# Turning the gated product on VectorE in 32 x 32 blocks instead of by fp32 transposes on TensorE, and projecting it with matmuls of 32 rows by 32 columns

## The chip, the cores and the metric

One core of one Trainium2 chip runs the whole kernel. The metric is the device time in microseconds from the first to the last instruction of that core with what lies around them. The median of three runs before the change is 772.9 us (772.75 to 773.51).

## The reference

Two layers of the same form run one after the other over x of shape (4, 32, 128, 128), with weights of their own:

```
def layer(x, W_in, W_dw, fft_weight, W_out):      # x is the group-normed input, one group per channel
    xm = einsum('bchw,oc->bohw', x, W_in)           # 32 -> 3 * 85 channels
    x_spatial, x_freq, x_gate = split(xm, 3, axis=1)
    out_spatial = depthwise_conv3x3(x_spatial, W_dw)
    out_freq = irfft2(rfft2(8x8 patches of x_freq) * fft_weight)
    x_fused = gelu(x_gate) * (out_spatial + out_freq)
    return einsum('bchw,oc->bohw', x_fused, W_out)  # 85 -> 32 channels
x = x + layer(gn(x), ...)    # layer 0
x = x + layer(gn(x), ...)    # layer 1
```

The change touches only the last lines of a layer: the product `x_fused`, which lies with pixels on the partitions, has to be turned so that its 85 channels lie there, and is then contracted with `W_out`, whose result is added to x.

## The kernel before

The image is cut in four bands of 32 columns (Q = 4), which lie with their 32 channels on the 128 partitions: partition 32 q + c is channel c of band q. A strip is 8 columns wide and 128 rows high; layer, batch and strip give 32 strips. A tile is 16 x 8 = 128 pixels of each band, 8 tiles to a strip, 256 in all. The engines walk through the same `steps()`, one tile to a step, with a prologue and a drain, and each engine has its order written out by hand in its own block; semaphores named `s_...` join them. Nothing plans the order at run time.

In step i TensorE does, in this order (L584 to L656): `conv(i, 0)` (seven matmuls that project and convolve band 0 of tile i, into one of two banks `ps_s`), the four fp32 transposes of tile i-2 into bank `ps_ft` (L594), every fourth step the output projection of four tiles (L616), the gate matmuls (L549) mixed with the other three bands' convolutions (L543), `turn` and `transform` of a later pair of tiles for the spectrum (L511, L523, L524), the projection of the spectrum of tile i+2 (`ps_z`, L639), and at the end two inverse-transform matmuls that complete the sum of tile i (L654, L656).

VectorE in step i: the product of the gate `g` and the sum in `ps_s` for tile i-1 (L1097, it signals `s_f`), in every fourth step the low part of a group's spectrum (L1045), in steps of certain numbers a normalization (L1005) or the low half of a strip's operands (`lo_part`, L1029, which waits for ScalarE's high half, L707), the weighting of the spectrum of tile i+2 (`y32`, L1120, needs `s_z`), and in every fourth step the residual sum out of `ps_o` (L1133), in layer 0 with statistics behind it (L967). ScalarE copies `ps_ft` to SBUF (L765, into one of 8 slots of `turned_results`), does the gelu (L770), moves the turned pixels (L727), makes the high half of `y32` (L777) and the high halves of the operands (L707). GpSimd makes the low half of `y32` (L844) and issues the DMAs that bring the spectrum into its stacked layout (`load_spectrum`, three DMAs for each of four bands q per group of four tiles, L425). SyncE issues the loads of the stacked operands.

TensorE waits for `s_f` of tile i-2 before `conv(i, 0)` since `ps_s` has two banks, for `s_y` of tile i+1 before `ps_z` is written, and for `s_gelu` of tile i-1 before the gate. The projection takes `wo` (85 x 32, fp32) as the stationary operand and four tiles of 128 pixels (512 columns) as the moving one, once per band, with band q's result in partitions 32 q to 32 q + 31 of `ps_o`. The factor `osc` that undoes the scaling of the weights is applied in the residual sum.

Of the kernel before, what the change touches and what calls it, by code (L numbers as in the profile page):

```python
# [47 lines left out]
PAIR, GROUP = 2, 4  # L48

# [49 lines left out]
def build(nc, x_in, edges_in, w_raw, w_fft, w_out, waves, squares, fold, sums, y_out):  # L99
    ctx = ExitStack()  # L100
    with ctx:
# [27 lines left out]
        turned_results = sb("turned_results", [128, 2 * OUT * Q * 128])  # L129
        raw = [turned_results[:, 0:12 * HID], yo[1][:, 0:12 * HID]]  # L130

        last = turned_results[0:KH, (2 * OUT - 1) * Q * 128:]
        fold_sb, fft = last[:, 0:128], [last[:, 128 + HID * i:128 + HID * (i + 1)] for i in range(LAYERS)]
        ones = turned_results[0:3, (2 * OUT - 1) * Q * 128 + 384:2 * OUT * Q * 128]
# [16 lines left out]
        wo = [sb(f"wo{i}", [HID, C]) for i in range(LAYERS)]  # L151
# [26 lines left out]
        ft = turned_results[0:HID, :].rearrange("p (t q n) -> p t q n", q=Q, n=128)  # L178
# [4 lines left out]
        ps_xt, ps_x, ps_g, ps_z, ps_ft, ps_o = (bank(n) for n in ("ps_xt", "ps_x", "ps_g", "ps_z", "ps_ft", "ps_o"))  # L183
# [10 lines left out]
        s_wo = sem("s_wo")  # L194
        s_x0 = [sem(f"s_x0_{i}") for i in range(STRIPS)]
# [51 lines left out]
        s_xs = [sem(f"s_xs{i}") for i in range(HELD)]  # L247
        s_z = sem("s_z")
# [7 lines left out]
        s_ftp = sem("s_ftp")  # L256
        s_ft = sem("s_ft")
        s_o = sem("s_o")
        s_res = sem("s_res")
# [179 lines left out]
        def _(sp):  # L439
# [7 lines left out]
            for l in range(LAYERS):  # L447
                sp.dma_start(wo[l][:, :], w_out[l]).then_inc(s_wo, 16)
# [19 lines left out]
        def _(pe):  # L468
# [24 lines left out]
            pe.wait_ge(s_wo, 16 * LAYERS)  # L493
            pe.wait_ge(s_id16, 1)

            def warm(n):

                for _ in range(n):
                    mm(ps_ft[:, 0:256], bas, waves_sb[:, :, :].rearrange("p a n -> p (a n)"), start=True, stop=True)
# [53 lines left out]
            def spectra_loaded(h):  # L553
# [3 lines left out]
                elif h == 1:  # L557
                    for by in range(2):
                        pe.wait_ge(s_xs_first[1][by], 16 * 2 * 3)
                else:  # L560
                    pe.wait_ge(s_xs[h % HELD], 16 * 3 * Q * ((h - 2) // HELD + 1))
# [22 lines left out]
            for i in steps():  # L584
# [21 lines left out]
                if live(i, -6) and i % OUT == 2:  # L606
# [52 lines left out]
        def _(act):  # L659
# [70 lines left out]
            def hi_of_spectrum(h):  # L730
# [5 lines left out]
                elif h > 3:  # L736
                    act.wait_ge(s_xs[(h - 2) % HELD], 16 * 3 * Q * ((h - 4) // HELD + 1))
# [65 lines left out]
        def _(pool):  # L803
# [28 lines left out]
            for i in steps():  # L832
# [3 lines left out]
                for h in range((i + 4) // GROUP, (i + 7) // GROUP + 1):  # L836
                    for q in range(Q):
# [19 lines left out]
        def _(dve):  # L857
# [24 lines left out]
            def scales(l):  # L882
# [10 lines left out]
                v.tensor_scalar(osc[l][:, :], p2[:, l, 0:1], p2[:, l, 1:2], 1.0 / SS, ALU.mult, ALU.mult)  # L893
# [155 lines left out]
            v.memset(ones[:, :], 1.0)  # L1049
            link(v.memset(amax[:, :, :], 0.0))  # L1050
# [197 lines left out]
```

## Time and profile before

| | |
|---|---|
| median of three runs | 772.9 us (772.75 to 773.51) |
| profiled execution, its own time | 775.2 us |
| its span, first to last instruction | 773.4 us |
| mean granted TensorE clock | 0.985 |
| TensorE matmuls busy | 723.6 us, 94% |
| VectorE busy | 545.1 us, 70% |
| ScalarE busy | 572.5 us, 74% |
| GpSimd busy | 624.1 us, 81% |

Busy time is the union of the engine's instructions. Neighbouring instructions of one engine overlap by some tens of ns in the records, because the next one starts while the one before still drains; so the distance between two starts says what an instruction costs in a row of others, and its duration what it costs to one that waits for its result.

### The profile page before, as it was taken

To read this page: it belongs to the slowest core of one execution; us is meant where nothing else is said; L and a number is where in the kernel's file an instruction comes from. 1 tells how busy PE (TensorE), PEld (TensorE's weight loads), DVE (VectorE), ACT (ScalarE), POOL (GpSimd) and SP (SyncE) were. 2 spreads that over 40 slices of the span, in tenths; PEclk is the share of its full clock that TensorE was granted. 3 is DMA by queue.
4 is the path that set the end of the run, shared out by engine and by line. 5 is a ranking of instruction groups with operands and counts; after the bars stand their busy time and mean duration, and the time that the engine had idled before them with its cause. 6 is when DMAs were issued, how large, how long until landed. Compare 5 with 4: busy or idle time off the path is not lost.

```text
span 773.4 us, 32267 instructions
## 1 busy us (share of the span) xinstructions
PE 723.6 (94%) x12324; PEld 620.0 (80%) x12324; DVE 545.1 (70%) x957; ACT 572.5 (74%) x1087; POOL 624.1 (81%) x1071
## 2 busy tenths in 40 slices
PE   2589989999999999999999999999999999999997
PEld 1477778877888878888788888889888988898875
DVE  7578867878877876777777687666666676667543
ACT  1676667777787778878887778787778777877754
POOL 1977777888888898888888987988788888988871
PEclk9689999999999999999999999999999999999999
DMA  8676888787767765677766766877767777787741
GB/s 299 162 182 174 195 181 211 170 190 174 180 177 191 182 160 152 163 167 182 189 171 165 166 183 176 216 190 199 190 176 192 194 199 204 194 209 191 191 129 56
DMA packets 96259, 140.61 MB, mean 182 GB/s; under 512 B 32498, under 2 KB 34746, under 8 KB 95978
## 3 DMA queue, kind: packets, MB, share of 16 engines
q1 hardware_dynamic: 64390, 103.30, 51.6%
q0 software_dynamic: 25376, 26.75, 14.1%
q10 hardware_dynamic: 6340, 8.49, 4.3%
q8 instruction: 99, 1.62, 1.0%
q14 instruction: 54, 0.44, 0.2%
HBM read 10.81 MB, written 8.54 MB: 25 GB/s over the span
## 4 chain that ended last, share of the span: by engine, by line
PE 72%; DVE 7%; issue 6%; POOL 6%; DMA 5%; ACT 2%; SPq 1%; ACTq 0%; POOLq 0%; DVEq 0%
PE ps_s L543 29%; PE ps_ft L594 12%; PE ps_o L616 7%; PE ps_g L549 5%; DMA xs<-xf 4%; PE ps_z L639 4%; PE ps_s L656 4%; PE ps_s L654 4%; PE ps_xt L511 3%; POOL xs L425 2%; PE ps_x L523 2%; PE ps_x L524 2%; POOL yl L844 1%; DVE y L1120 1%; POOL stack L305 1%
## 5 line engine op out<-in xcount | busy, mean ns | idle before, releaser
L543 PE MATMUL ps_s<-cw,stack 128*128 128x85 f16 (+1 forms) x7168 | 407.3, 203 | 1.8 <-DMA stack<-parts 1.6
L425 POOL DMA_DIRECT2D xs<-xf x757 | 385.2, 513 | 15.7 <-PE ps_z L639 12.5
L543 PEld LDWEIGHTS ps_s<-cw,stack 128*128 128x128 f16 (+1 forms) x7168 | 352.8, 99 | 27.4 <-issue 1.9
L844 POOL TENSOR_TENSOR yl<-y,yh 128x340 f16<-128x340 f32 x256 | 219.0, 856 | 105.2 <-ACT yh L777 103.1
L1120 DVE TENSOR_TENSOR y<-ps_z,weff 128x340 f32<-128x340 f32 x256 | 129.6, 506 | 136.8 <-PE ps_z L639 129.9
L777 ACT ACTIVATE yh<-y 128x340 f16<-128x340 f32 x256 | 124.6, 487 | 135.2 <-DVE y L1120 118.1
L1029 DVE TENSOR_TENSOR parts<-xn,parts 128x1024 f16<-128x1024 f32 (+2 forms) x99 | 126.9, 1284 | 63.8 <-ACT parts L707 63.5
L594 PE MATMUL ps_ft<-squares_sb,g 128*85 128x128 f32 x1024 | 163.4, 282 | 0.8 <-ACT turned_results L765 0.8
L765 ACT ACTIVATE turned_results<-ps_ft 85x512 f32<-85x512 f32 x256 | 149.3, 583 | 16.7 <-issue 10.0
L770 ACT ACTIVATE g<-ps_g,gsc 128x340 f32<-128x340 f32 x256 | 137.2, 536 | 18.7 <-PE ps_g L549 18.2
L1097 DVE TENSOR_TENSOR g<-ps_s,g 128x340 f32<-128x340 f32 x256 | 128.2, 501 | 11.0 <-PE ps_s L656 8.1
L549 PEld LDWEIGHTS ps_g<-pw,stack 128*128 128x128 f16 x1024 | 82.6, 98 | 55.2 <-issue 52.8
L549 PE MATMUL ps_g<-pw,stack 128*128 128x85 f16 x1024 | 125.0, 205 | 0.0
L594 PEld LDWEIGHTS ps_ft<-squares_sb,g 128*85 128x85 f32 x1024 | 115.3, 155 | 2.1 <-DVE g L1097 1.0
L707 ACT ACTIVATE parts<-xn 128x1024 f16<-128x1024 f32 (+2 forms) x99 | 100.3, 1017 | 14.4 <-DVE xn L1013 12.4
L639 PE MATMUL ps_z<-pw,xs 96*128 96x85 f16 x1024 | 81.5, 203 | 12.4 <-DMA xs<-xf 12.0
L654 PE MATMUL ps_s<-yh,waves 128*128 128x340 f16 x256 | 79.7, 311 | 0.0
L727 ACT ACTIVATE xt<-ps_xt 128x512 f16<-128x512 f32 x127 | 74.7, 588 | 6.7 <-PE ps_xt L511 4.2
L656 PE MATMUL ps_s<-yl,waves 128*128 128x340 f16 x256 | 79.0, 309 | 0.6 <-POOL yl L844 0.6
L616 PE MATMUL ps_o<-turned_results,wo 85*32 85x512 f32 x512 | 68.2, 605 | 1.3 <-ACT turned_results L765 0.7
L639 PEld LDWEIGHTS ps_z<-pw,xs 96*128 96x128 f16 x1024 | 54.9, 98 | 14.2 <-DMA xs<-xf 7.1
L523 PE MATMUL ps_x<-waves,xt 128*128 128x128 f16 x254 | 42.9, 222 | 13.7 <-DVE xf L1045 10.4
(108 smaller groups left out, 548.0 us busy)
## 6 DMA issues: line engine op xcount, KB each, us to landing
stack<-parts SPq DMA_DIRECT2D x496, 130.0 KB, 3.6
xs<-xf POOLq DMA_DIRECT2D x757, 32.0 KB, 2.8
out_y<-yo SPq DMA_DIRECT2D x16, 512.0 KB, 3.1
stack<-parts SPq DMA_DIRECT2D x93, 64.5 KB, 2.9
stack<-parts SPq DMA_DIRECT2D x93, 64.0 KB, 2.8
x<-in_x SPq DMA_DIRECT2D x16, 256.0 KB, 6.0
stack<-parts ACTq DMA_DIRECT2D x62, 65.0 KB, 3.8
stack<-parts SPq DMA_DIRECT2D x62, 65.0 KB, 2.8
```

The source lines that it names most:

```text
L425: eng.dma_start(xs[C * k:C * k + C, h % HELD, q, :], xf[C * q:C * q + C, h % 2, SPECTRA[k], :]).then_inc(loaded, 16)
L543: mm(ps_s[i % 2][:, HID * q:HID * (q + 1)], pixels(kind, i, q, dy, rows), w[0:rows, m, :], start=(q == 0 and m == 0), stop=False)
L549: t = mm(ps_g[:, HID * q:HID * (q + 1)], pixels(A, i, q, 0), pw[layer(i)][:, 1, :], start=(q == 0), stop=(q == Q - 1))
L594: t = nc.tensor.transpose(ps_ft[0:HID, q * 128:(q + 1) * 128], g[:, k, HID * q:HID * (q + 1)], id32)
L639: z = mm(ps_z[:, HID * q:HID * (q + 1)], xs[:, (i + 2) // GROUP % HELD, q, col:col + 128], pw[layer(i + 2)][0:3 * C, 0, :], start=(q == 0) ...
L765: nc.scalar.activation(ft[:, (i - 2) % (2 * OUT), :, :].rearrange("p q n -> p (q n)"), ps_ft[0:HID, 0:Q * 128], ACT.Copy).then_inc(s_ft, 1)
L770: nc.scalar.activation(g[:, i % 2, :], ps_g[:, 0:GC], ACT.Gelu, scale=gsc[layer(i)][:, 0:1]).then_inc(s_gelu, 1)
L777: nc.scalar.activation(yh[:, i % 2, :], y32[:, i % 2, :], ACT.Copy).then_inc(s_yh, 1)
L844: nc.gpsimd.tensor_tensor(yl[:, k, :], y32[:, k, :], yh[:, k, :], ALU.subtract).then_inc(s_yl, 1)
L1029: v.tensor_tensor(part[:, LO, rows], xn[:, rows, 1 + dx:1 + dx + TW], part[:, HI, rows], ALU.subtract).then_inc(s_xl, 1)
L1097: v.tensor_tensor(g[:, k, :], ps_s[k][:, 0:GC], g[:, k, :], ALU.mult).then_inc(s_f, 1)
L1120: v.tensor_tensor(y32[:, k, :].rearrange("p (q o) -> p q o", q=Q), ps_z[:, 0:GC].rearrange("p (q o) -> p q o", q=Q), weff[layer(i + 2)][:, ...
```

## The change

The product goes to a buffer `f` of its own, whose rows are padded from 85 to 96 = 3 x 32 channels. VectorE turns it there in square blocks of 32 x 32 into `ft` and signals `s_ft`; the four fp32 transposes, bank `ps_ft` and ScalarE's copy are gone. Each 32-row group of `ft` then holds 32 channels of one block for 32 pixels, so the output is projected by matmuls of 32 rows and 32 columns: two bank halves, three blocks that are summed, four bands, and two rounds n between which TensorE waits for its own first round (`s_o_half`). `W_out` is laid out anew on the host in blocks and repeated four times, the factor `osc` goes into it once (`s_wo_scaled`), the residual sum becomes two plain additions, one per bank. The fourth of the four band loads of the spectrum is issued by ScalarE instead of GpSimd.

```diff
@@ TensorE
-                if live(i, -2):
-                    k = i % 2
-                    need(pe, s_f, i - 1)
-                    need(pe, s_ft, i - 2)
-                    for q in range(Q):
-                        t = nc.tensor.transpose(ps_ft[0:HID, q * 128:(q + 1) * 128],
-                                                g[:, k, HID * q:HID * (q + 1)], id32)
-                    t.then_inc(s_ftp, 1)
...
-                    for q in range(Q):
-                        o = mm(ps_o[C * q:C * q + C, :], wo[layer(tile)][:, :], ft[:, k:k + OUT, q, :],
-                               start=True, stop=True)
-                    o.then_inc(s_o, 1)
+                    if tile % LT == 0:
+                        pe.wait_ge(s_wo_scaled, layer(tile) + 1)
+                    for n in range(2):
+                        if n == 1:
+                            pe.wait_ge(s_o_half, tile // OUT + 1)
+                        for block in range(BLOCKS):
+                            for half in range(2):
+                                rows = slice(BLOCK * (2 * half + n), BLOCK * (2 * half + n + 1))
+                                out = ps_os[half][:, 0:OUT * 2 * BLOCK].rearrange("p (t n x) -> p t n x", n=2, x=BLOCK)
+                                for q in range(Q):
+                                    o = mm(out[C * q:C * q + C, :, n, :], wo[layer(tile)][rows, block, :],
+                                           ft[rows, k:k + OUT, q, block, :],
+                                           start=(block == 0), stop=(block == BLOCKS - 1))
+                        o.then_inc((s_o_half, s_o)[n], 1)
@@ ScalarE
-                if live(i, -2):
-                    need(act, s_ftp, i - 1)
-                    need(act, s_o, (i - 2 - 2 * OUT) // OUT + 1)
-                    nc.scalar.activation(ft[:, (i - 2) % (2 * OUT), :, :].rearrange("p q n -> p (q n)"), ps_ft[0:HID, 0:Q * 128],
-                                         ACT.Copy).then_inc(s_ft, 1)
                 if live(i, 0):
                     need(act, s_gate, i + 1)
-                    need(act, s_ftp, i - 1)
+                    need(act, s_f, i - 1)
...
+                for h in range(2, GROUPS_OF_TILES):
+                    if loads_at(h, Q - 1) == i:
+                        load_spectrum(act, h, Q - 1, s_xs_act[h % HELD])
@@ GpSimd
-                    for q in range(Q):
+                    for q in range(Q - 1):
@@ VectorE
+                dve.wait_ge(s_wo, 16 * LAYERS)
+                v.tensor_scalar(wo[l], wo[l], osc[l][:, 0:1], None, ALU.mult).then_inc(s_wo_scaled, 1)
...
-                    v.tensor_tensor(g[:, k, :], ps_s[k][:, 0:GC], g[:, k, :], ALU.mult).then_inc(s_f, 1)
+                    v.tensor_tensor(f[:, k, :, 0:HID], ps_s[k][:, 0:GC].rearrange("p (q o) -> p q o", q=Q),
+                                    g[:, k, :].rearrange("p (q o) -> p q o", q=Q), ALU.mult).then_inc(s_f, 1)
                 if i in leaving:
                     lo_of_spectrum(leaving[i])
+                if live(i, -1):
+                    dve.wait_ge(s_f, i)
+                    need(dve, s_o, (i - 1 - 2 * OUT) // OUT + 1)
+                    v.transpose(ft[:, (i - 1) % (2 * OUT), :, :, :].rearrange("p q b n -> p (q b n)"),
+                                f[:, (i - 1) % 2, :, :].rearrange("p q h -> p (q h)")).then_inc(s_ft, 1)
...
-                    v.scalar_tensor_tensor(xv if l + 1 < LAYERS else staging,
-                                           ps_o[:, :].rearrange("p (r w) -> p r w", w=TW),
-                                           osc[l][:, 0:1], xv, ALU.mult, ALU.add).then_inc(s_res, 1)
+                    for half in range(2):
+                        ...
+                        o = v.tensor_tensor(new, ps_os[half][...], old, ALU.add)
+                    o.then_inc(s_res, 1)
```

## Rows read from the trace of the kernel before

**Rows 1.** Page, part 1: busy us (share of the span) xinstructions of each engine.
```profile
PE 723.6 (94%) x12324; PEld 620.0 (80%) x12324; DVE 545.1 (70%) x957; ACT 572.5 (74%) x1087; POOL 624.1 (81%) x1071
```
**Rows 2.** Page, part 4: the chain of waits, share of the span by engine.
```profile
PE 72%; DVE 7%; issue 6%; POOL 6%; DMA 5%; ACT 2%; SPq 1%; ACTq 0%; POOLq 0%; DVEq 0%
```
**Rows 3.** Busy time by stretch: length, PE, PEld, DVE, ACT, POOL, PE clock, DMA.
```profile
58.30:227.80 169.50, 158.77 (x2700) 135.35 (x2696) 134.66 (x241) 123.90 (x235) 136.22 (x236) 0.99 0.79 187
227.80:409.30 181.50, 177.24 (x3077) 152.30 (x3074) 134.94 (x230) 145.59 (x279) 157.26 (x268) 1.00 0.69 169
409.30:584.90 175.60, 173.27 (x3027) 149.87 (x3024) 121.97 (x201) 136.08 (x260) 149.12 (x255) 1.00 0.72 187
584.90:760.00 175.10, 173.94 (x3056) 150.33 (x3054) 110.15 (x186) 132.63 (x254) 143.73 (x246) 1.00 0.69 185
```
**Rows 4.** Timeline of PE, 404.99 to 409.37: start, us, group.
```profile
404.99 0.45 PE L543 MATMUL ps_s<-cw,stack 128*128 128x85 f16 x7
405.27 0.64 PE L594 MATMUL ps_ft<-squares_sb,g 128*85 128x128 f32 x4
405.75 0.24 PE L549 MATMUL ps_g<-pw,stack 128*128 128x85 f16 x2
...
407.71 0.64 PE L594 MATMUL ps_ft<-squares_sb,g 128*85 128x128 f32 x4
408.28 1.07 PE L616 MATMUL ps_o<-turned_results,wo 85*32 85x512 f32 x8
409.28 0.25 PE L549 MATMUL ps_g<-pw,stack 128*128 128x85 f16 x2
```
**Rows 5.** Timeline of PE again, cut off at 408.31 us.
```profile
408.28 0.64 PE L616 MATMUL ps_o<-turned_results,wo 85*32 85x512 f32 x4
```
**Rows 6.** Timeline of DVE, 399.88 to 402.81 us.
```profile
399.88 0.74 DVE L1133 SCALAR_TENSOR_TENSOR x<-ps_o,osc,x 128x512 f32<-128x512 f32 x1
400.66 0.69 DVE L967 BATCH_NORM_STATS2 st<-x 128x6 f32<-128x512 f32 x1
401.27 0.49 DVE L1097 TENSOR_TENSOR g<-ps_s,g 128x340 f32<-128x340 f32 x1
401.68 1.22 DVE L1029 TENSOR_TENSOR parts<-xn,parts 128x1024 f16<-128x1024 f32 x1
402.81 0.50 DVE L1120 TENSOR_TENSOR y<-ps_z,weff 128x340 f32<-128x340 f32 x1
```
**Rows 7.** One DVE line: ns min/median/max of each form.
```profile
L925 DVE COPY cw<-vh x1: 294/294/294, 24.2 to 24.2; 96x510 f16<-96x510 f16 x1
```
**Rows 8.** Waits, 58.3 to 227.8: engine line, releaser: us, times, longest.
```profile
DVE y L1120 <- PE ps_z L639: 21.3, 18, 3.3
DVE parts L1029 <- ACT parts L707: 10.4, 13, 1.2
```
**Rows 9.** Waits, 227.8 to 409.3 us.
```profile
DVE parts L1029 <- ACT parts L707: 13.9, 16, 1.1
```
**Rows 10.** Waits, 409.3 to 584.9 us.
```profile
DVE parts L1029 <- ACT parts L707: 19.0, 22, 1.1
```
**Rows 11.** Waits, 584.9 to 760 us.
```profile
DVE y L1120 <- PE ps_z L639: 44.4, 37, 3.4
DVE parts L1029 <- ACT parts L707: 17.2, 19, 1.1
```
**Rows 12.** Lines of ACT and POOL: xcount, busy us, mean ns, idle before.
```profile
L765 ACT ACTIVATE turned_results<-ps_ft 85x512 f32<-85x512 f32 x256 | 149.3, 583 | 16.7 <-issue 10.0 <-PE ps_ft L594 4.6 <-PE ps_o L616 1.7
L425 POOL DMA_DIRECT2D xs<-xf x757 | 385.2, 513 | 15.7 <-PE ps_z L639 12.5 <-issue 2.3 <-ACT xf L738 0.7
```
**Rows 13.** DMA issues, 130 to 730 us: KB each, median us to landing.
```profile
xs<-xf POOLq DMA_DIRECT2D x642, 32.0 KB, 2.8
stack<-parts ACTq DMA_DIRECT2D x54, 65.0 KB, 3.7
```
**Rows 14.** Timeline of ACT and its queue at 403.4 us.
```profile
403.35 0.49 ACT L777 ACTIVATE yh<-y 128x340 f16<-128x340 f32 x1
403.41 0.51 ACTq L311 DMA_DIRECT2D stack<-parts  x1
```
**Rows 15.** Page, part 5: the convolution's matmuls as a group.
```profile
L543 PE MATMUL ps_s<-cw,stack 128*128 128x85 f16 (+1 forms) x7168 | 407.3, 203 | 1.8 <-DMA stack<-parts 1.6
```

More of the change, by code:

```diff
@@ L48 @@
 PAIR, GROUP = 2, 4
+BLOCK = 32
+BLOCKS = -(-HID // BLOCK)
 HELD = 3
@@ L126, in build @@
         own = sb("own", [128, Q])
-        turned_results = sb("turned_results", [128, 2 * OUT * Q * 128])
+        turned_results = sb("turned_results", [128, 2 * OUT * Q * BLOCKS * BLOCK])
         raw = [turned_results[:, 0:12 * HID], yo[1][:, 0:12 * HID]]
-        last = turned_results[0:KH, (2 * OUT - 1) * Q * 128:]
+        last = turned_results[0:KH, (2 * OUT - 1) * Q * BLOCKS * BLOCK:]
         fold_sb, fft = last[:, 0:128], [last[:, 128 + HID * i:128 + HID * (i + 1)] for i in range(LAYERS)]
-        ones = turned_results[0:3, (2 * OUT - 1) * Q * 128 + 384:2 * OUT * Q * 128]
+        ones = sb("ones", [3, 128])
         win = [r[:, 0:3 * HID] for r in raw]
@@ L150, in build @@
         weff = [sb(f"weff{i}", [128, HID]) for i in range(LAYERS)]
-        wo = [sb(f"wo{i}", [HID, C]) for i in range(LAYERS)]
+        wo = [sb(f"wo{i}", [128, BLOCKS, C]) for i in range(LAYERS)]
         gsc = [sb(f"gsc{i}", [128, 1]) for i in range(LAYERS)]
@@ L177, in build @@
             "p (a b n) -> p a b n", a=PAIR, b=2)]
-        ft = turned_results[0:HID, :].rearrange("p (t q n) -> p t q n", q=Q, n=128)
+        f = sb("f", [128, 2, Q, BLOCKS * BLOCK])
+        ft = turned_results[:, :].rearrange("p (t q b n) -> p t q b n", q=Q, b=BLOCKS, n=BLOCK)
         def bank(name):
@@ L182, in build @@
         ps_s = [bank("ps_s0"), bank("ps_s1")]
-        ps_xt, ps_x, ps_g, ps_z, ps_ft, ps_o = (bank(n) for n in ("ps_xt", "ps_x", "ps_g", "ps_z", "ps_ft", "ps_o"))
+        ps_xt, ps_x, ps_g, ps_z = (bank(n) for n in ("ps_xt", "ps_x", "ps_g", "ps_z"))
+        ps_os = [bank("ps_o0"), bank("ps_o1")]
+        ps_o = ps_os[0]
         turned = [ps_g[0:3, 0:128], ps_o[0:3, 0:128]]
@@ L194, in build @@
         s_wo = sem("s_wo")
+        s_wo_scaled = sem("s_wo_scaled")
         s_x0 = [sem(f"s_x0_{i}") for i in range(STRIPS)]
@@ L247, in build @@
         s_xs = [sem(f"s_xs{i}") for i in range(HELD)]
+        s_xs_act = [sem(f"s_xs_act{i}") for i in range(HELD)]
         s_z = sem("s_z")
@@ L255, in build @@
         s_f = sem("s_f")
-        s_ftp = sem("s_ftp")
         s_ft = sem("s_ft")
         s_o = sem("s_o")
+        s_o_half = sem("s_o_half")
         s_res = sem("s_res")
@@ L498, in warm @@
                 for _ in range(n):
-                    mm(ps_ft[:, 0:256], bas, waves_sb[:, :, :].rearrange("p a n -> p (a n)"), start=True, stop=True)
+                    mm(ps_os[1][:, 0:256], bas, waves_sb[:, :, :].rearrange("p a n -> p (a n)"), start=True, stop=True)
             def turn(p):
@@ L560, in spectra_loaded @@
                 else:
-                    pe.wait_ge(s_xs[h % HELD], 16 * 3 * Q * ((h - 2) // HELD + 1))
+                    pe.wait_ge(s_xs[h % HELD], 16 * 3 * (Q - 1) * ((h - 2) // HELD + 1))
+                    pe.wait_ge(s_xs_act[h % HELD], 16 * 3 * ((h - 2) // HELD + 1))
             def stacks_loaded(tile, kind):
@@ L1049, in _ @@
             v.memset(ones[:, :], 1.0)
+            v.memset(f[:, :, :, HID:], 0.0)
             link(v.memset(amax[:, :, :], 0.0))
@@ L1132, in _ @@
                     staging = yo[k % 2][:, TW * row:TW * (row + OUT * TH)].rearrange("p (r w) -> p r w", w=TW)
-                    v.scalar_tensor_tensor(xv if l + 1 < LAYERS else staging,
-                                           ps_o[:, :].rearrange("p (r w) -> p r w", w=TW),
-                                           osc[l][:, 0:1], xv, ALU.mult, ALU.add).then_inc(s_res, 1)
+                    for half in range(2):
+                        old, new = (r.rearrange("p (t s r) w -> p t s r w", t=OUT, s=2)[:, :, half, :, :]
+                                    for r in (xv, xv if l + 1 < LAYERS else staging))
+                        o = v.tensor_tensor(new, ps_os[half][:, 0:OUT * 2 * BLOCK].rearrange(
+                            "p (t r w) -> p t r w", t=OUT, w=TW), old, ALU.add)
+                    o.then_inc(s_res, 1)
                     if l + 1 < LAYERS:
@@ L1234 @@
         arrays[f"w_fft{l}"] = np.ascontiguousarray(raw["fft_weight"].reshape(HID, -1).T)
-        arrays[f"w_out{l}"] = np.ascontiguousarray(raw["W_out"].T)
+        w_out = np.zeros((BLOCKS * BLOCK, C), np.float32)
+        w_out[0:HID] = raw["W_out"].T
+        arrays[f"w_out{l}"] = np.ascontiguousarray(np.tile(w_out.reshape(BLOCKS, BLOCK, C).transpose(1, 0, 2), (128 // BLOCK, 1, 1)))
     arrays.update(constants())
```

10 lines of the change are left out of this document (6 added, 4 removed).

## The prediction

> **What bounds the kernel now.** I read the busy shares first, then the chain of waits, the stretches, the waits of VectorE and at last single steps. TensorE is busy 94% of the span, the next is GpSimd with 81% [rows 1], and the chain that ended last runs over TensorE for 72% [rows 2]. The stretches show that this is no average of unlike stages: from 227.8 us on TensorE is busy 177.2 of 181.5, 173.3 of 175.6 and 173.9 of 175.1 us, at the full granted clock; only the first stretch (seven strips) has 10.7 us of idle TensorE in it [rows 3]. Each later stretch is 64 tiles, 16 groups of four. So what goes from TensorE goes from the time, until another engine is reached. The reader should look at which that is: VectorE has 35, 47, 54 and 65 us free per stretch, and part of it isn't free, since it waits there for ScalarE's half of an operand (10.4, 13.9, 19.0 and 17.2 us) [rows 8 to 11].
>
> **TensorE, removed.** In a step the four transposes take from 405.27 to the next matmul at 405.75, 0.48 us [rows 4]. The projection: the transposes ahead of it start at 407.71 and would be followed at 408.19; the next matmul of another kind starts at 409.28. That is 1.09 us per group, of which the eight records begin only at 408.28, 0.09 late [rows 4]. Per group of four tiles: 4 x 0.48 + 1.09 = 3.01 us.
>
> **TensorE, added.** 2 rounds x 3 blocks x 2 halves x 4 bands = 48 fp32 matmuls. The four of before are 8 records, so an fp32 matmul is two passes: 96 passes with 96 weight loads per group. Four records begin within 0.03 us of each other with 0.64 us each [rows 5], and the eight end after 1.07 [rows 4]: matmuls in different columns of 32 run side by side, and the second set of passes adds 0.43 us. What a pass over 128 fp32 columns costs in its own corner of the array isn't shown; 0.43 / 4 = 0.11 by the projection, 0.12 by the transposes, four in 0.48 [rows 4]. I take 0.12. No row shows two groups of 32 rows at work at once. Bounds: fully beside each other, a round is 3 blocks x 2 passes x 0.12 = 0.72 us; in succession 1.44. I take them as side by side, since that is how the columns behave, plus one pass of 0.12 for the whole as skew. Between the rounds TensorE waits for its own last matmul: the tail of a record behind its stream is 0.64 - 0.43 = 0.21 us, and a result reaches the next instruction of the same engine 0.04 us late (below), 0.25 together; everything else of TensorE is queued behind that wait. Entering and leaving cost what they cost before: 1.09 - 2 x 0.43 = 0.23. Sum: 0.23 + 2 x 0.72 + 0.12 + 0.25 = 2.04 us. Bounds: 1.9 without skew, 3.5 if the halves go in succession (0.23 + 2.88 + 0.25 + 0.12). The four tiles' transposed operands come from VectorE at least one step ahead of the projection, so no new wait there.
>
> Net per group: 2.04 - 3.01 = -0.97 us; 14 groups in the first stretch, 16 in each other, 64 in all, -62 us if nothing else were reached. TensorE's time then: 169.5 - 13.6 = 155.9 (its waits of before kept), 181.5 - 15.5 = 166.0, 175.6 - 15.5 = 160.1, 175.1 - 15.5 = 159.6.
>
> The trace bounds the price of a single small pass only from above: the convolution has 7168 matmuls in 407.3 us of busy time, 0.057 each where others lie between, and seven in a row take 0.28 us (404.99 to 405.27), 0.040 each with their weight loads, at 85 columns [rows 4, 15]; the four records of rows 5 are far closer. The Trainium skill (TensorE: Matmul & The Clock Gate, "Wait — 56ns, not 53.3ns?") says that start-to-start never drops below about 25 ns however few columns a matmul has. By that page, as an estimate, 96 passes take 2.4 us instead of 1.56, the group 2.9 and the net is -0.1. The four records within 0.03 us [rows 5] don't agree with it where the columns differ.
>
> **VectorE, added.** One turn of 384 fp32 elements per partition in each step. The trace has no such instruction. The product with 340 elements takes 0.49 and starts 0.41 before its successor; statistics over 512 take 0.69 [rows 6]. At (0.69 - 0.49) / 172 = 1.2 ns per element the turn takes 0.49 + 0.05 = 0.54, in a row 0.46. Bounds: 0.21 by the copy of 510 16-bit elements in 0.294 [rows 7], 0.95 if it needs two cycles per element. I take 0.46, by the nearest rows. In addition it waits for the product just ahead: the statistics, which wait for the sum ahead of them, start 0.04 us after its end (399.88 + 0.74 to 400.66), where an instruction without such a wait starts 0.08 before it (401.27 + 0.49 to 401.68) [rows 6]; 0.12 us in three of four steps, since L1045 stands between in the fourth. Together 0.46 + 0.09 = 0.55 per tile: 31 us in the first stretch, 35 in each other. The residual becomes two additions of 256 elements: 0.66 before in a row, 2 x (0.49 - 84 x 0.0012 - 0.08) = 0.62 after; nothing. Behind the turn stands everything of that step, the operand halves, `y32` and through it TensorE's next `ps_z`.
>
> Part of it is hidden: where the product is followed by L1029, VectorE waits 0.8 to 0.9 us for ScalarE's half (10.4 / 13, 13.9 / 16, 19.0 / 22, 17.2 / 19) [rows 8 to 11], and the turn lies in that wait. That leaves about 0.3 us each: 3, 5, 6, 6 us. VectorE's time: 134.7 + 31 + 3 = 169; 134.9 + 35 + 5 = 175; 122.0 + 35 + 6 = 163; 110.2 + 35 + 6 = 151 [rows 3].
>
> **ScalarE and GpSimd.** ScalarE loses 0.58 us per tile (149.3 in all) and GpSimd a quarter of its spectrum DMAs, 385.2 / 4 = 96 us of issue [rows 12]. Neither was the bound, so this is worth nothing by itself; it makes ScalarE's gelu and high halves earlier. The moved loads: three DMAs of 0.51 us of queue time each every four steps. On ScalarE the queue's issue lies beside a running activation (403.41 beside the 403.35 one) [rows 14], but they now stand behind that step's L777, which waits for VectorE's `y32`, and are used by `ps_z` two steps on. Landing takes 2.8 us from GpSimd, 3.7 from ScalarE's queue with larger pieces [rows 13]: 0.1 + 3 x 0.51 + 3.7 = 5.3 us behind that `y32`, against two TensorE steps with a projection between, 2.0 + 4.0 less 0.9 of the first. It is close to late; if VectorE is ahead it costs some tenths per group. I count nothing, and up to 0.3 x 60 = 18 us in the range.
>
> **Together.** The larger of both times per stretch: 169, 175, 163, 160, sum 667 against 701.7, -35. An engine that is behind in one step isn't always made good in the next: the projection gives TensorE a step of 4 us while VectorE has its long steps elsewhere, and neither can run more than about a step ahead. I add 1% of 702, 7 us. Prologue: the scaling of `wo` and the clearing of padding, 0.5 us on VectorE (the like of L925, 0.29 [rows 7]). -27.5 us. The profiled execution took 775.2 (span 773.4 and 1.8 around it), so 747.5; the median of the runs was 2.3 lower, 745.
>
> **Rivals.** (a) TensorE becomes slower: the group of small passes costs more than the 3.01 us removed. The point is a round of 1.2 us, or 26 ns per pass. If the two row groups don't run together, the group takes 3.5, +0.5 x 64 = 32 us, and as TensorE stays the bound nearly all of it shows: about 805; at the convolution's 0.040 per pass 96 x 0.040 + 0.6 = 4.4, +1.4 x 64 = 92, about 865. For it: 96 small instructions with a weight load each have never been seen in succession. Against: rows 5. Chance 0.18. (b) VectorE's turn at two cycles per element, 0.95 instead of 0.46: +27 in the first stretch and +31 in the others on VectorE's times, 196, 206, 194, 182, sum 778, 76 above before: about 850, slower too. Chance 0.06. (c) A pass has a floor of its own that lies above what its stream needs in a corner of the array: a round takes 1.15 us, between the 0.72 taken and the 1.9 of 48 passes at the convolution's 0.040. The group is 2.9, TensorE's times are 168, 180, 174, 174, and with VectorE's 169 in the first stretch the sum is 697: -5 to -8, about 767. For it: no more than 16 small instructions in succession are in the trace. Against: rows 5. The Trainium skill's 25 ns (same page and section as above) would be this case. Chance 0.12. (d) VectorE and TensorE fit together worse than I add, by waits for the late spectrum loads or lost steps, 10 to 20 us: 755 to 765. Chance 0.14; with it the change brings little though each price holds. (e) The change is hidden better: VectorE's waits for `ps_z` (21.3 us in the first stretch, 44.4 in the last [rows 8, 11]) take the turn, no loss by fit: 730 to 738. Chance 0.12. The forecast itself, 738 to 755: 0.38. That no transposes leave TensorE can't be.
>
> **How the numbers follow.** About 1.5 us, 0.2%, is what a measurement here tells from no change. Slower by more: (a), (b) and a small part of (d), 0.26. Within: 0.04, out of (c) and (d). Faster: the rest, 0.70. The range holds the forecast, (c), (d), (e) and the near end of (a): 728 to 805. The forecast's own range is 738 to 755.
>
> **What would show it.** L616's group should last about 1.6 us of stream and the next gate matmul start about 2.0 us behind the convolution's last; a round should be 0.7 to 0.8 us, and at its records the two halves should start together. The turn should read 0.54 us. VectorE should be busy about 90% and more in the first two stretches, with its waits for `ps_z` nearly gone there, and TensorE idle 5 to 10% there and little in the last stretch, where most of the gain should be: per stretch 0, -6, -12, -14 us. If the two halves' records follow each other, (a) holds; if the turn reads near 1 us, (b). TensorE waiting for `xs` DMAs in every group shows the late loads.

## The result

The changed kernel takes 841.2 us (median of four runs, 838.0 to 847.0), the kernel before 773.2 us beside it: a ratio of 1.088 [1.084, 1.092]. I had forecast 745, with 728 to 805 as the range; it lies outside, on the slow side. The profiled execution took 840.2 us (span 838.1). Of the 96 us between forecast and result, the experiments below give 41 to the moved loads of the spectrum and 27 to the steps in which VectorE's other work stands; 28 stay open.

Page of the changed kernel, parts 1 and 4, against [rows 1, 2]:

```profile
PE 693.5 (83%) x16932; PEld 599.8 (72%) x16932; DVE 671.8 (80%) x1280; ACT 446.8 (53%) x831; POOL 529.4 (63%) x885
PE 46%; DVE 24%; issue 16%; ACT 4%; ACTq 3%; POOL 3%; SPq 2%; DMA 1%; DVEq 0%; POOLq 0%
```

TensorE is no longer the bound, and nothing has taken its place: 83% and 80% busy, and a chain that changes from one to the other. The stretches (length, busy time of PE, PEld, DVE, ACT, POOL, then PE clock, DMA share, GB/s), cut behind the groups of projections 0, 14, 30, 46 and 62 of 64:

```profile
59.90:251.80 191.90, 158.61 (x3710) 136.10 (x3704) 161.30 (x310) 95.43 (x176) 113.94 (x192) 0.93 0.68 166
251.80:451.70 199.90, 170.07 (x4225) 146.31 (x4225) 168.00 (x312) 115.22 (x216) 130.76 (x219) 0.97 0.64 155
451.70:640.90 189.20, 163.96 (x4228) 143.21 (x4224) 153.59 (x283) 107.30 (x200) 128.45 (x211) 1.00 0.70 177
640.90:828.00 187.10, 164.37 (x4180) 144.38 (x4181) 140.91 (x267) 99.48 (x188) 120.40 (x197) 0.97 0.65 170
```

By the projection's records the same tiles take 169.5, 181.5, 179.0 and 174.1 us in the kernel before (its cuts in [rows 3] differ from these by some us in the last two). Each stretch is 10 to 22 us longer, and in none is an engine busy more than 88%. The two priced instructions are what I took them for, in the timeline of PE and in the page's groups:

```profile
399.73 1.95 PE L629 MATMUL ps_o<-turned_results,wo 32*32 32x128 f32 x96
401.60 0.25 PE L559 MATMUL ps_g<-pw,stack 128*128 128x85 f16 x2
```
```profile
L1122 DVE STREAM_TRANSPOSE turned_results<-f 128x384 f32<-128x384 f32 x256 | 147.4, 576 | 6.6
```

So the time is in waits. Of the changed kernel's waits, those that lead on (us in total, times, longest; GpSimd's `yl`, 267.9 us, and ScalarE's high half `yh`, 187.0 us, wait longest of all, each for the engine ahead of it):

```profile
DVE y L1144 <- PE ps_z L653: 94.1, 68, 5.8
ACT g L780 <- PE ps_g L559: 52.5, 55, 3.5
ACT g L780 <- issue: 50.5, 52, 3.2
PE ps_x L533 <- DVE xf L1062: 46.5, 59, 1.7
PE ps_z L653 <- issue: 24.1, 27, 2.6
PEld ps_z L653 <- issue: 33.9, 31, 6.2
DVE f L1115 <- ACT g L780: 22.5, 21, 2.6
```

Two are new: ScalarE's gelu stands 50.5 us for nothing but "issue", and TensorE's `ps_z` 24.1 us. A third has grown: TensorE waits 46.5 us for the low part of the spectrum, 10.4 before. The first two are explained by the moved loads. Line L436 on ScalarE's queue (ns min/median/max), and its timeline in one step:

```profile
L436 ACTq DMA_DIRECT2D xs<-xf x186: 514/549/2300, 57.7 to 816.3; - x186
```
```profile
459.18 0.49 ACT L787 ACTIVATE yh<-y 128x340 f16<-128x340 f32 x1 [0.98 <-DVE y L1144]
459.43 0.52 ACTq L436 DMA_DIRECT2D xs<-xf  x1
459.58 1.04 ACT L721 ACTIVATE parts<-xn 128x1024 f16<-128x1024 f32 x1
460.05 1.20 ACTq L436 DMA_DIRECT2D xs<-xf  x2
461.34 0.54 ACT L780 ACTIVATE g<-ps_g,gsc 128x340 f32<-128x340 f32 x1 [0.73 <-PE ps_z L653]
```

The split of 1.04 us ends at 460.62, but the gelu starts only at 461.34, behind the third issue. (The view puts its idle time down to `ps_z`, on which L780 doesn't wait; the gate and the product that it needs were done by 460.04.) Behind it come TensorE's next gate, VectorE's product and everything after that.

The second is the loads' landing. On the first tile of a group `ps_z` needs ScalarE's three loads, and as the view has no landing for them it says "issue":

```profile
488.95 0.20 PEld L653 LDWEIGHTS ps_z<-pw,xs 96*128 96x128 f16 x4 [0.89 <-issue]
```

The semaphore records of the trace have the landings. In 32 of the 62 groups this weight load starts 0.06 us behind the last landing of ScalarE's loads, after 0.07 to 2.7 us of idle time, 27.5 us in all.

To see where TensorE loses its time I averaged, over steps 64 to 189, the distance between successive starts of the last matmul of a step (L670), by the step's place in the group of four. Place 0 holds the transform, place 2 the projection:

```
                  place 0   1      2      3     sum
before             2.77   2.44   3.62   2.44   11.3
after              3.59   2.01   4.54   2.03   12.2
e1 loads back      3.57   2.04   4.04   1.98   11.6
f1 back, low       3.31   2.01   4.17   1.98   11.5
g1 rounds split    3.22   3.02   3.19   1.97   11.4
h1 one block       3.80   2.05   3.40   1.99   11.2
j1 staging moved   3.13   1.97   4.09   2.01   11.2
k1 and halves      2.92   2.09   4.05   2.02   11.1
k3 and short turn  2.70   2.03   4.12   2.01   10.9
k2 before, moved   2.46   2.54   3.58   2.44   11.0
```

Places 1 and 3 fell by 0.4 us, as they should (a step less its 0.48). Place 0, 2.3 by the forecast's terms (2.77 less 0.48), rose to 3.6; place 2, forecast at 4.0, stands at 4.5. Place 2 is where the first tile's `ps_z` stands: it takes 5.03 us in the 15 groups of this stretch that wait for the loads and 4.10 in the 16 that don't.

### The profile page after: what moved, and what is told of

It reads as the page before. It is cut to its first block, busy times and chain, and to the rows that moved or that the text cites. A ratio compares the mean times of both kernels' runs of the same rounds, so it can differ in the third digit from the quotient of the medians.

```text
span 838.1 us, 41297 instructions
## 1 busy us (share of the span) xinstructions
PE 693.5 (83%) x16932; PEld 599.8 (72%) x16932; DVE 671.8 (80%) x1280; ACT 446.8 (53%) x831; POOL 529.4 (63%) x885
## 4 chain that ended last, share of the span: by engine, by line
PE 46%; DVE 24%; issue 16%; ACT 4%; ACTq 3%; POOL 3%; SPq 2%; DMA 1%; DVEq 0%; POOLq 0%
PE ps_s L553 17%; PE ps_o L629 12%; DVE f L1115 5%; DVE y L1144 5%; DVE xf L1062 4%; PE ps_g L559 3%; PE ps_z L653 3%; PE ps_s L670 2%; PE ps_s L668 2%; DVE x L1160 2%; PE ps_x L533 2%; PE ps_xt L521 2%; ACTq L322 2%; ACT g L780 2%; SPq L316 2%
## 5 line engine op out<-in xcount | busy, mean ns | idle before, releaser
L553 PEld LDWEIGHTS ps_s<-cw,stack 128*128 128x128 f16 (+1 forms) x7168 | 361.2, 101 | 40.4 <-DVE f L1115 17.1
L858 POOL TENSOR_TENSOR yl<-y,yh 128x340 f16<-128x340 f32 x256 | 216.3, 846 | 269.1 <-ACT yh L787 267.9
L436 POOL DMA_DIRECT2D xs<-xf x571 | 295.8, 522 | 8.4 <-issue 6.2
L787 ACT ACTIVATE yh<-y 128x340 f16<-128x340 f32 x256 | 124.6, 487 | 210.1 <-DVE y L1144 187.0
L780 ACT ACTIVATE g<-ps_g,gsc 128x340 f32<-128x340 f32 x256 | 138.5, 541 | 146.7 <-PE ps_g L559 52.5
L1122 DVE STREAM_TRANSPOSE turned_results<-f 128x384 f32<-128x384 f32 x256 | 147.4, 576 | 6.6
L1115 DVE TENSOR_TENSOR f<-ps_s,g 128x340 f32<-128x340 f32 x256 | 129.4, 506 | 26.7 <-ACT g L780 22.5
L559 PE MATMUL ps_g<-pw,stack 128*128 128x85 f16 x1024 | 127.9, 209 | 11.5 <-ACT g L780 10.3
L1046 DVE TENSOR_TENSOR parts<-xn,parts 128x1024 f16<-128x1024 f32 (+2 forms) x99 | 118.1, 1194 | 23.8 <-ACT parts L721 23.6
L629 PE MATMUL ps_o<-turned_results,wo 32*32 32x128 f32 x6144 | 121.0, 274 | 11.1 <-PE ps_o L629 3.4
L653 PE MATMUL ps_z<-pw,xs 96*128 96x85 f16 x1024 | 83.7, 206 | 43.6 <-issue 24.1
L629 PEld LDWEIGHTS ps_o<-turned_results,wo 32*32 32x32 f32 x6144 | 85.6, 103 | 34.2 <-PE ps_o L629 24.3
L559 PEld LDWEIGHTS ps_g<-pw,stack 128*128 128x128 f16 x1024 | 73.4, 101 | 28.9 <-ACT g L780 18.2
L533 PE MATMUL ps_x<-waves,xt 128*128 128x128 f16 x254 | 44.2, 227 | 48.4 <-DVE xf L1062 46.5
L670 PE MATMUL ps_s<-yl,waves 128*128 128x340 f16 x256 | 81.1, 317 | 0.9 <-POOL yl L858 0.7
L533 PEld LDWEIGHTS ps_x<-waves,xt 128*128 128x128 f16 x254 | 24.9, 100 | 55.9 <-issue 53.0
```

What stands on the lines that cost most here:

```text
L436: eng.dma_start(xs[C * k:C * k + C, h % HELD, q, :], xf[C * q:C * q + C, h % 2, SPECTRA[k], :]).then_inc(loaded, 16)
L553: mm(ps_s[i % 2][:, HID * q:HID * (q + 1)], pixels(kind, i, q, dy, rows), w[0:rows, m, :], start=(q == 0 and m == 0), stop=False)
L559: t = mm(ps_g[:, HID * q:HID * (q + 1)], pixels(A, i, q, 0), pw[layer(i)][:, 1, :], start=(q == 0), stop=(q == Q - 1))
L629: o = mm(out[C * q:C * q + C, :, n, :], wo[layer(tile)][rows, block, :], ft[rows, k:k + OUT, q, block, :], start=(block == 0), stop=(block ...
L653: z = mm(ps_z[:, HID * q:HID * (q + 1)], xs[:, (i + 2) // GROUP % HELD, q, col:col + 128], pw[layer(i + 2)][0:3 * C, 0, :], start=(q == 0) ...
L780: nc.scalar.activation(g[:, i % 2, :], ps_g[:, 0:GC], ACT.Gelu, scale=gsc[layer(i)][:, 0:1]).then_inc(s_gelu, 1)
```

## The experiments

All times are medians; the kernel before ran beside each batch (772.9 to 774.0 us).

**The loads: e1, h2, f3.** e1 gives the fourth band's loads back to GpSimd, nothing else:

```diff
-    for h in range(2, GROUPS_OF_TILES):      # ScalarE
-        if loads_at(h, Q - 1) == i:
-            load_spectrum(act, h, Q - 1, s_xs_act[h % HELD])
-    for q in range(Q - 1):                   # GpSimd
+    for q in range(Q):
```

> The changed kernel with the fourth band's spectrum loads issued by GpSimd again (as before). Theory A (no engine is the bound; the cost is a ring of waits through VectorE, ScalarE and TensorE, of which ScalarE's DMA issue is one link: gelu waited 50.5 us in 52 places behind it): 841 falls to 800-820. Theory B (the ring runs only over VectorE's order: product, turn, low parts, y32): 835-842, no change. Theory C (more TensorE stalls feed more of the low granted clock, whatever the loads do): as B.

799.8 us, 1.032 [1.029, 1.036]: the loads cost 41 us. h2 leaves them on ScalarE, one DMA in each of three steps (two steps and one step ahead of the old place, and at it):

```diff
-    if loads_at(h, Q - 1) == i:
+    if h < 4 and loads_at(h, Q - 1) == i:
         load_spectrum(act, h, Q - 1, s_xs_act[h % HELD])
+    if h >= 4 and 0 <= i - loads_at(h, Q - 1) + 2 < 3:
+        load_row(act, h, Q - 1, i - loads_at(h, Q - 1) + 2, s_xs_act[h % HELD])
```

> The changed kernel with its loads left on ScalarE, but the three DMAs of a group spread over three steps (one in each of the two steps before, and one in the step where all three stood). Theory A (three issues in a row of one step hold the gelu for 2 us, and one issue fits into a step's free time of ScalarE): most of the 41 us that the loads cost comes back, 800-815. Theory B (each issue costs its 0.55 us wherever it stands): 835-845.

803.8, 1.039 [1.036, 1.042]: 37 of the 41 us come back though every DMA is still ScalarE's, with the same bytes on the same queue. What costs is three issues in succession at this place, and it costs in two ways, which h2 takes away together: the gelu waits 12.8 us for issues instead of 50.5, and TensorE's `ps_z` waits 1.7 us on "issue" instead of 24.1. No run separates them. That place 2 takes 4.10 us in the groups that don't wait for the loads and 4.04 in e1 points to the late landing for much of the 41, but this is argued, not tried. f3 moves the same loads in the kernel before:

> The kernel before with only the fourth band's spectrum loads moved from GpSimd to ScalarE. Theory A (the issue holds ScalarE's gelu for about 2 us in every fourth step, and that costs whatever else is changed): 30-50 us above before, 803-823. Theory B (it costs only where VectorE has no room left): 0-10 us above.

852.9, 1.103 [1.099, 1.106]: the edit that I counted as nothing costs 79 us alone, more than the whole change. There the late landing is small (6 groups, 3.5 us); what stands behind the issues on ScalarE is the copy of `ps_ft`, for which TensorE waits 65.9 us (0.8 before), and the gelu:

```profile
PEld ps_ft L596 <- issue: 72.2, 62, 2.6
PE ps_ft L596 <- ACT turned_results L768: 65.9, 62, 2.5
DVE g L1104 <- ACT g L773: 51.4, 55, 2.3
ACT turned_results L768 <- issue: 41.6, 45, 2.9
```

**VectorE's order and the price of the turn: e2, e3, e4, f1, f2, f4.** e2 puts the low part of the spectrum at the end of the step before; e3 puts the turn behind `y32`; e4 turns one band of four and leaves the output of the other three stale.

```diff
-    if i in leaving:
+    if i + 1 in leaving and leaving[i + 1] >= 4:      # e2, f1: at the end of the step
         lo_of_spectrum(...)
-    turn                                              # e3: from behind the product ...
+    turn                                              # ... to behind y32
+    bands = Q if i - 1 < 2 * OUT else 1               # e4, f2: ft[..., 0:bands], f[..., 0:bands]
```

> The changed kernel with the low part of a group's spectrum (L1062) made at the end of VectorE's step before, behind y32 and the residual, instead of behind the next product. TensorE's transform waited for it 46.5 us in 59 places. Theory A (that wait ties the two engines in every fourth step and no longer lets TensorE run ahead): 15-40 us faster than 841. Theory B (the wait only takes the place of the next one, for y32 or the product): within 5 us of 841.

> The changed kernel with the turn put behind y32 in VectorE's step instead of ahead of the low parts and y32. The work of VectorE is the same, less 0.12 us of wait for the product per step. Theory A (the turn costs because it stands in the ring product - low parts - y32 - spectrum projection): 20-50 us faster than 841, and TensorE waits less for y32. Theory B (VectorE's work as such is what costs, wherever it stands): 0-10 us faster.

> The changed kernel with only one of four bands turned from the ninth tile on (96 instead of 384 columns; the output of the other bands is then left from earlier tiles). It takes 288 columns, about 0.3 us, from VectorE per step, 76 us in all, at the same place. Theory A or B of the turn (VectorE's time stands in the ring): 841 falls by 50-80 us, to 760-790. If the projection's own stall and clock are the cause: it falls by under 20.

e2 844.0, 1.088 [1.082, 1.094], nothing, although TensorE's wait for the low part fell from 46.5 to 17.8 us: in its place the gelu's wait on issues rose from 50.5 to 67.7 and `ps_z`'s from 24.1 to 42.1, so TensorE ran into the late loads instead. e3 868.1, 1.123 [1.118, 1.127], 27 us slower: a miss of the theory that `y32` should come first. e4 826.2, 1.065 [1.060, 1.070]: only 15 us for 74 us less of turns on VectorE, which by what I had written down speaks against VectorE's time as such. With the loads back, f1 and f2 repeat e2 and e4:

> The changed kernel with the fourth band's loads on GpSimd again (800 by itself) and the low part of the spectrum at the end of VectorE's step before. TensorE's wait for it was 46.6 us there. Theory A (with ScalarE's issue out of the way this is the next link that ties TensorE to VectorE's step): 765-785. Theory B (the wait only moves to y32 and the product, since VectorE's time per step is what counts): 795-803.

> The changed kernel with the loads on GpSimd again and one band of four turned (96 instead of 384 columns, so three bands of the output are left from earlier tiles). Theory A (what is left of the loss, 27 us, is VectorE's time): it falls from 800 by 35 to 60 us, to 740-765. Theory C (the packed projection or its clock holds TensorE): it falls by under 10.

f1 787.6, 1.018 [1.014, 1.022], 12 under e1 (the wait for the low part 20.4 us); f2 781.9, 1.009 [1.006, 1.012], 18 under e1. The low part's place was worth nothing while the loads hid it. f4 adds to the kernel before, in the turn's place, a statistic over 384 elements with the turn's wait and no user:

> The kernel before with one more VectorE instruction of 384 elements per step, of the turn's length (0.55 us against the turn's 0.58), waiting for the product, in the turn's place; its result is not used. TensorE's work stays. Theory A (VectorE's time at this place costs by itself): 20-50 us above 773. Theory B (with TensorE's steps as long as before, VectorE has room for it): under 8 us above.

791.4, 1.023 [1.020, 1.025]: 17 us from VectorE alone, busy 70% before, and TensorE's wait for the low part rises from 10.4 to 26.1 us. VectorE at 70% had no free room in the steps where it mattered.

**The projection: g1, g2, h1.** g1 (on f1) and g2 (on e1) put the first round of small passes one step earlier; h1 (on e1) projects one block of three and leaves the other two out of the output.

```diff
+    if live(i, -5) and i % OUT == 1 and i - 5 != 2 * OUT:   # g1, g2
+        project(i - 5, 0)                                   # round 1 stays in the old step
-    for block in range(BLOCKS):                             # h1
+    for block in range(1):
```

> The changed kernel with the loads on GpSimd, the spectrum's low part a step earlier (788 by these two), and the two rounds of the projection in two steps of TensorE instead of one. TensorE then has steps of 2, 3, 3, 2 us in place of 2, 2, 4, 2. Theory A (what is left is the fit of the two engines' steps: TensorE's 4 us step falls on a light one of VectorE's): 735-765, faster than both kernels. Theory B (VectorE's own steps fill the time, 11.4 us per group wherever TensorE's stand): 782-790.

> The changed kernel with the loads on GpSimd (800) and the two rounds in two steps, without the earlier low part. Theory A of the fit: 765-785. Theory B: 795-802.

> The changed kernel with the loads on GpSimd (800) and one of three blocks of the projection (two blocks of channels are left out of the output): 32 of 96 passes, 1.1 us less TensorE work per group, 70 us in all. If TensorE's time were what is left: it falls by 50-70. If VectorE's steps set the time: by under 20. Theory A of the fit, in which TensorE's long step costs beside a light one of VectorE: by 25-50.

g1 786.2, 1.016 [1.011, 1.021], as f1; g2 806.4, 1.041 [1.036, 1.047], 7 us above e1. Spreading the burst and taking away the wait between its rounds gave nothing in either; in g1's row of the table TensorE's work is even and place 0 still takes 3.2. h1 770.4, 0.996 [0.994, 0.999]: TensorE's busy time falls from 681.2 to 628.2 us, the time by 29, so about half of what TensorE is relieved of reaches the time. All of it is in place 2; place 0 even grows, 3.57 to 3.80.

**The late step: j1, j2, j3, k1, k2, k3.** In e1's timeline of PE, DVE and ACT a step of place 3 and the next of place 0 (L1156 is the residual, L980 the statistics, L1018 a normalisation, L1058 the low part):

```profile
437.05 0.51 DVE L1140 TENSOR_TENSOR y<-ps_z,weff 128x340 f32<-128x340 f32 x1 [0.93 <-PE ps_z L653]
437.22 0.31 PE L670 MATMUL ps_s<-yl,waves 128*128 128x340 f16 x1
...
437.48 0.75 DVE L1156 TENSOR_TENSOR x<-ps_o,x 128x256 f32<-128x256 f32 x2
...
438.25 0.69 DVE L980 BATCH_NORM_STATS2 st<-x 128x6 f32<-128x512 f32 x1
...
438.87 0.49 DVE L1111 TENSOR_TENSOR f<-ps_s,g 128x340 f32<-128x340 f32 x1
...
439.39 0.58 DVE L1118 STREAM_TRANSPOSE turned_results<-f 128x384 f32<-128x384 f32 x1
...
439.90 0.91 DVE L1018 TENSOR_SCALAR xn<-x,mv,rstd 128x1280 f32<-128x1280 f32 x1
...
440.72 0.51 DVE L1140 TENSOR_TENSOR y<-ps_z,weff 128x340 f32<-128x340 f32 x1
441.14 0.51 DVE L1111 TENSOR_TENSOR f<-ps_s,g 128x340 f32<-128x340 f32 x1
...
441.29 0.33 PE L653 MATMUL ps_z<-pw,xs 96*128 96x85 f16 x4 [0.40 <-DVE y L1140]
441.56 0.69 DVE L1058 SCALAR_TENSOR_TENSOR xf<-ps_x,xf 128x512 f16<-128x512 f32 x1
...
442.39 0.22 PE L533 MATMUL ps_x<-waves,xt 128*128 128x128 f16 x1 [0.78 <-DVE xf L1058]
```

VectorE waits 0.93 us for `ps_z` in the step with the projection, then works without a pause for 5 us, and TensorE waits twice in place 0 for its results. The free time and the work stand in different steps. `even`, the edit of j1 (on e1), j2 (on f1) and j3 (on the kernel before), moves two of a strip's four pieces from places 3 into places 2, ahead of the `y32` that waits there, with ScalarE's half of one of them; k1 and k2 also make ScalarE's halves a step earlier; k3 is k1 with the short turn.

```diff
-    strip, mine = staged(i, {0: 0, 2: 2, 4: 4, 6: 6}, ...)    # VectorE
+    strip, mine = staged(i, {2: 2, 3: 4, 6: 6}, ...)
+    ahead = (i + 2) // TPS + 2
+    if i % TPS == TPS - 2 and ahead < ALL and ahead != STRIPS:
+        norm(ahead)
-    staged(i, {1: 1, 3: 3, 5: 5}, ...)                        # ScalarE
+    staged(i, {1: 1, 2: 3, 5: 5}, ...)                        # k1, k2, k3: {0: 1, 1: 3, 4: 5}
```

> The changed kernel with the spectrum loads back on GpSimd (799.8 us), and of every strip's staging on VectorE two of the four pieces moved by one step: the normalisation from the steps i%8==7 to the steps before, the middle split from i%8==3 to i%8==2 (ScalarE's half of it one step earlier too). Same work. Theory L (a late step): VectorE's step i can begin only with TensorE's end of step i-1 and must be through when TensorE's step i+1 wants its y32. For VectorE's steps i%4==3 that window is a short TensorE step (2.0) and the first 1.2 us of a step without projection, 3.3 us, for 3.7 us of work; the loss shows in TensorE's steps i%4==0, which take 3.55 for 2.3 us of their own. With the heavy pieces in i%4==2, whose window holds the projection, steps i%4==0 fall to 2.4 to 2.9 us: 0.6 to 1.1 us x 64 = 40 to 70 us, 730 to 760. Theory S (the work's sum and the latencies of the ring set the time, wherever the work stands): TensorE's steps i%4==2 take up what i%4==0 gives, 790 to 805.

> The same staging edit on the kernel with the loads back and the low part of the spectrum at the end of the step before (787.6 us). Theory L: the low part now again stands at the end of the steps i%4==3, but these have 1.2 us less work; 725 to 755, below the run without it by some us. Theory S: 780 to 795.

> The same staging edit on the kernel before (773). Theory L: without the turn VectorE's steps i%4==3 hold 3.3 us of work in a window of 2.44 + 1.4 = 3.8 us, nothing is late there and TensorE's steps i%4==0 take what they hold (2.79): 768 to 778. Theory S: the same. It says whether the edit has a worth of its own: if it gives 20 us or more here, what it gives in the changed kernel is not the turn's doing.

j1 772.7, 0.999 [0.997, 1.001], 27 us under e1 with the same work, so the sum of the work does not set the time. The gain stands in place 0, 3.57 to 3.13, 0.44 us in 64 groups. But I expected 40 to 70, and place 0 still takes 3.1. j2 776.3, 1.004 [1.002, 1.006]: the low part's early place no longer helps. j3 767.4, 0.992 [0.989, 0.995]: 5.5 us, a fifth of what the edit gives beside the turn. Three waits of j1, to set beside 23.4, 46.6 and 76.0 us in e1:

```profile
DVE parts L1042 <- ACT parts L721: 34.5, 68, 0.8
PE ps_x L533 <- DVE xf L1058: 24.1, 41, 1.6
DVE y L1143 <- PE ps_z L653: 23.6, 20, 5.8
```

VectorE's time in front of `y32` is used (76.0 to 23.6), and TensorE's wait for the low part is halved.

> As j1 (772.7 us), with ScalarE's halves of the staging one step earlier as well, since VectorE waits for them 34.5 us in j1. Theory L: VectorE's steps i%4==1 and 2 get shorter by these waits, of which some half stand where TensorE waits for VectorE: 10 to 20 us less, 753 to 763, below the kernel before. Rival: ScalarE's steps i%8==7 and 0 become too full and its gelu late for TensorE's gate: 770 to 785.

> Both edits of the staging in the kernel before (j3: 767.4 us with the first alone). TensorE is the bound there and waits little for VectorE: 762 to 768. If it is below k1, transposes on TensorE remain the better choice; if k1 is below, the turn on VectorE pays once the staging is moved.

> k1 with only one of four bands turned from the ninth tile on (three bands of the turned results are left out), 74 us less of work on VectorE. If after the moved staging VectorE is the bound, 30 to 50 us less than k1; if the ring's latencies and TensorE are, 10 to 20 (18 without the staging edit).

k1 771.0, 0.997 [0.995, 1.000]: 2 us for 34.5 us of waits, a miss. The rival's range holds it, but not its mechanism: TensorE's gate waits 3.9 us for the gelu, 2.4 in j1. VectorE's waits for the halves are gone and its split is slower instead. Over all three forms that is 1506 ns against 1327 in j1 and 1194 in the changed kernel; of 1024 elements alone, 1.56 us against 1.37 and 1.23:

```profile
L1042 DVE TENSOR_TENSOR parts<-xn,parts 128x1024 f16<-128x1024 f32 (+2 forms) x99 | 148.9, 1506 | 2.0 <-ACT parts L721 1.9
```

k3 758.4, 0.981 [0.978, 0.984]: 12.5 us under k1, not the 30 to 50 of a bound on VectorE, though VectorE is busy 91% in k1. k2, the kernel before with the two staging edits, takes 765.2, 0.989 [0.987, 0.991]: of the kernels that leave nothing out it is the fastest, faster than the kernel before and the changed one. The transposes on TensorE remain the better choice here.

## Why the prediction was wrong

**TensorE, removed and added: right.** The 48 fp32 matmuls are 96 passes, and from the convolution's last matmul to the next gate it is 2.03 us in the median group against 2.04. Within a round 48 starts lie in 0.667 us (forecast 0.72), and the halves run side by side. Rival (a) is out. So is (c): 14 ns from start to start on average, 6 to 7 within a set of eight. That 25 ns is a floor, as the Trainium skill has it (TensorE: Matmul & The Clock Gate, "Wait — 56ns, not 53.3ns?"), doesn't hold for fp32 passes in corners of 32 x 32. (The break-even round of 1.2 us in rival (a) is 25 ns per pass, not 26.) Of the 62 us TensorE's busy time shows only 30, 54 in j1; part of the rest is the lower clock, below.

**VectorE, added: right.** 0.576 us against 0.54. Rival (b) is out. The Trainium skill (Vector Engine (DVE) Microarchitecture Reference, "3.8 The reshape front-end and per-opcode configuration") says that the turn sustains one element per cycle per lane. The traces don't contradict it: 384 elements take 0.576 us and 96 (e4) 0.275, about 1.04 ns for each further one, where the rows before gave 1.2 for statistics; how long a cycle is, no row shows.

**ScalarE and GpSimd: the first step that failed.** "It is close to late; if VectorE is ahead it costs some tenths per group. I count nothing, and up to 0.3 x 60 = 18 us in the range." The move cost 41 us in this kernel, 79 alone in the kernel before, 4 when spread over three steps. The landing itself was sized right: 5.3 us behind `y32` in the forecast, 5.28 in the median group. To price it at nothing was wrong, for TensorE waits for it in 32 groups, 0.86 us each, 27.5 us. The second cost isn't in the sum at all: what stands behind the issues on ScalarE. [rows 14] show one issue beside a running activation, and that holds for one; of three in a row the last outlasts it, and the gelu behind them gates TensorE, VectorE and, through them, the next gelu. How the 41 us divide between the two isn't known; in the kernel before, the landing was 3.5 of the 79. The Trainium skill (DMA: Bandwidth & Descriptors, "Issuing engines are not separate DMA queues") says that issuing from several engines only saves the sequencer's time, "usually small relative to the DMA itself". The trace agrees with the ratio: 0.55 us for an issue on ScalarE, against 3.6 from the third issue's start to the landing. But three of them in a row at this place weren't small for the kernel, and nothing was gained on GpSimd's side: `yl` waited 267.9 us for ScalarE, where it waited 103.1 before.

**Together: the second.** "I add 1% of 702, 7 us" for the fit of both engines. With the loads back the kernel is at 799.8, not 745: 55 us for the fit and all else. 27 of them are shown to be the place of VectorE's staging (e1 to j1; 5.5 of these the edit gives without the turn too, j3), since a stretch's larger busy time says nothing about when an engine may work: VectorE can begin step i only behind TensorE's step i-1, and TensorE's next `ps_z` and transform need it. I had seen the mismatch and named it ("the projection gives TensorE a step of 4 us while VectorE has its long steps elsewhere"), yet priced it at 1%. Its signs failed with it: VectorE is busy 84% of each of the first two stretches, not 90%, and still waits 23.7 and 19.0 us for `ps_z` in them, and TensorE is idle 17% and 15%. The forecast of 0, -6, -12, -14 us by stretch came out as +22, +18, +10 and +13.

**What is left, 28 us between j1 and the forecast.** k3 shows that half of the turn's time is worth 12.5 of it in this order. The clock is a term that I left out: granted 0.960 in the changed kernel and 0.976 in j1 against 0.985. Between the levels of 1.2 and 2.4 GHz that is 2 x (1 - 0.960) x 838 = 67 us at the lower one, 37 in j1 and 23 before; in the first stretch it was 0.93 with TensorE busy 83%, and 0.99 before with 94%. At half speed the 44 us more cost up to 22, in j1 up to 7; this is worked out, no run separates it. What holds place 0 at 2.9 in k1 isn't settled. The slower splits and TensorE's waits for the product (21.5 us in j1) stand beside it, and no run tells them apart.

**The rivals.** (d) was the right kind, worse fit and late loads, at 10 to 20 us instead of some 95; the sign that I gave for it, TensorE waiting for `xs`, came in every second group. (e) had it backwards: VectorE's waits for `ps_z` fell in place 2 and the turn was needed in places 3 and 0.

## What to carry to other kernels

Work that leaves the bound engine for one with 30% free is worth what the receiving engine has free in the very steps where it must answer; lay both engines' work out by step of the period before adding busy times. DMA issues are instructions of the engine that issues them: several in a row hold back the operation behind them and land late, while the same ones, one per step and begun earlier, were nearly free. A transfer that by your own sum lands as late as it is needed has a price; put it into the sum. When an edit does nothing, look whether another wait covers it: the same move of the low part gave nothing with the loads in the way, 12 without them, and again nothing once the staging had moved.

## What the runs showed of the hardware

- fp32 matmuls of 32 rows and 32 columns start mostly 6 to 7 ns apart in different corners of the array, in sets of eight. From the last start of a set to the first of the next it is 59 ns in the median (83 behind the first set, 34 before the last); a round of 48 passes takes 0.93 us with its tail, and the second round, which waits for the first, starts 0.345 us behind the first one's last start.
- A DMA issued on ScalarE's queue takes 0.55 us in the median (0.51 to 2.3), and no activation that stands behind it in the program begins in it: of ScalarE's activations only the splits (58) and one high half, which stand ahead, begin during one of the 186 issues, and no gelu. The landing comes 3.6 us behind the start of the third issue in the median.
- The split of 1024 elements on VectorE, 1.23 us here, takes 1.56 us in k1 on the mean. In k1 the 53 that take over 1.5 us have GpSimd's `yl` beside them for 0.67 us on the mean, the 21 under 1.26 hardly at all. But in k2 73 short ones have it beside them for as long, so `yl` alone doesn't explain it.
- TensorE fetched its instructions in 134 transfers instead of 99. In the 6 us behind the start of such a transfer the idle share of its matmuls was at most 0.21 in any quarter of a microsecond and 0.15 on the mean, against 0.14 overall; no stall shows.
